# Mixture of experts on one Trainium2 core: the down product from three products of rounded parts in place of float32, and result rows kept in four buffers in place of two

## The reference, cut to what matters

```python
xbuf = jnp.zeros((E, C, D)).at[e_sorted, pos].set(x[tok_sorted], mode='drop')
g = jnp.einsum('ecd,efd->ecf', xbuf, w_gate)
u = jnp.einsum('ecd,efd->ecf', xbuf, w_up)
y = jnp.einsum('ecf,edf->ecd', jax.nn.silu(g) * u, w_down)
y_pair = y[e_sorted, safe_pos] * (s_sorted * valid)[:, None]
out = jnp.zeros((N, D)).at[tok_sorted].add(y_pair)
```

## Time and profile before

| | |
|---|---|
| median of three runs | 2299.77 us (2297.57 to 2302.56) |
| profiled execution, from its first to its last instruction | 2296.0 us |
| what lies around the span, taken as median less span | 3.8 us |
| TensorE busy, over the whole span | 2102.5 us (92%) |
| VectorE busy | 1751.3 us (76%) |
| ScalarE busy | 1441.0 us (63%) |
| POOL busy | 684.0 us (30%) |
| expert stage, from the first transpose to the start of the first load of the last stage | 1864.8 to 2242.9 us |

### The profile page before, as it was taken

The page is one execution under the profiler, slowest core; times in us unless marked ns, Lnnn a source line. Parts: engine busy times, 40 slices in busy tenths (PEclk is TensorE's granted clock), DMA queues, the critical chain, the costliest instruction groups (busy, mean ns, idle before and its releaser), DMA issues. The chain is left out here.

```text
span 2296.0 us, 56054 instructions
## 1 busy us (share of the span) xinstructions
PE 2102.5 (92%) x21448; PEld 1456.2 (63%) x21448; DVE 1751.3 (76%) x3728; ACT 1441.0 (63%) x3012; POOL 684.0 (30%) x646
## 2 busy tenths in 40 slices
PE   7999999999999999999999999999997149999975
PEld 5666666666666666666666666666664037777754
DVE  5557887979797978888888888797978736656646
ACT  2667676768676767676777767676867124444433
POOL 1002040404131322213130404040403427767770
PEclk9999999999999999999999999999999569999998
DMA  7586672323132313232323323232310136676648
GB/s 226 192 288 210 235 250 75 114 82 89 72 89 72 93 70 91 77 83 79 100 88 82 97 64 105 55 105 68 107 47 25 56 119 212 199 229 209 201 138 331
DMA packets 132711, 294.16 MB, mean 128 GB/s; under 512 B 21899, under 2 KB 89143, under 8 KB 126304
## 3 DMA queue, kind: packets, MB, share of 16 engines
q1 hardware_dynamic: 114016, 255.89, 35.7%
q0 software_dynamic: 18432, 34.69, 4.3%
HBM read 165.40 MB, written 108.27 MB: 119 GB/s over the span
## 5 line engine op out<-in xcount | busy, mean ns | idle before, releaser
L801 ACT ACTIVATE sb_probs<-S,sb_negmax 128x1604 f32<-128x1604 f32 x256 | 409.2, 1598 | 278.5 <-DVE sb_negmax L979 277.0
L793 ACT ACTIVATE sb_probsT<-W 128x384 f32<-128x384 f32 (+1 forms) x1024 | 473.6, 513 | 68.2 <-PE W L639 65.3
L639 PE MATMUL W<-sb_ident,sb_probs 128*128 128x128 f32 (+1 forms) x3328 | 478.3, 280 | 15.7 <-DVE sb_o_tok L992 8.0
L979 DVE TENSOR_REDUCE sb_negmax<-S 128x1 f32<-128x1604 f32 x256 | 466.2, 1821 | 2.9 <-PE S L629 1.2
L639 PEld LDWEIGHTS W<-sb_ident,sb_probs 128*128 128x128 f32 (+1 forms) x3328 | 363.5, 139 | 133.9 <-issue 64.7
L612 PE MATMUL W<-sb_wkv_in,sb_ctx 128*128 128x256 f32 (+1 forms) x1664 | 410.7, 389 | 14.2 <-ACT sb_probsT L793 6.6
L602 PE MATMUL W<-sb_ctx,sb_wkv_in 128*32 128x401 f32 x4096 | 399.3, 504 | 4.4 <-DVE sb_V L973 2.9
L612 PEld LDWEIGHTS W<-sb_wkv_in,sb_ctx 128*128 128x128 f32 (+1 forms) x1664 | 293.3, 187 | 79.1 <-ACT sb_probsT L793 25.7
L1335 POOL DMA_INDIRECT y_scratch<-sb_ys,sb_places x256 | 264.4, 1033 | 112.1 <-issue 109.0
L963 DVE SCALAR_TENSOR_TENSOR sb_K_lo<-W,sb_pair_cols,sb_K_hi 128x401 fp32r<-128x401 f32 x256 | 162.2, 633 | 175.5 <-ACT sb_K_hi L785 175.2
L785 ACT ACTIVATE sb_K_hi<-W,sb_pair_cols 128x401 fp32r<-128x401 f32 x256 | 153.2, 598 | 181.5 <-PE W L602 181.4
(11 more groups left out here) (188 smaller groups left out, 2921.0 us busy)
## 6 DMA issues: line engine op xcount, KB each, us to landing
sb_ctx<-ctxT SPq DMA_DIRECT2D x32, 1604.0 KB, 7.7
xe_scratch<-sb_none SPq DMA_DIRECT2D x32, 1088.0 KB, 12.7
sb_xg<-xe_scratch SPq DMA_DIRECT2D x64, 544.0 KB
sb_BC<-bc_scratch SPq DMA_DIRECT2D x32, 1024.0 KB, 5.9
sb_Q_hi<-sb_q_hi SPq DMA_DIRECT2D x128, 128.0 KB, 4.5
sb_Q_lo<-sb_q_lo SPq DMA_DIRECT2D x128, 128.0 KB, 5.4
y_scratch<-sb_none SPq DMA_DIRECT2D x16, 1024.0 KB, 12.0
sb_rows<-y_scratch SPq DMA_DIRECT2D x16, 1024.0 KB, 8.1
```

Source lines behind the costliest of these rows:

```text
L639: ins = pe.transpose(W[0:keys_in(t), at * P:(at + 1) * P], probs[n % 2][:, t * P:t * P + keys_in(t)], ident[:])
L793: act.activation(probsT[k][n % (k + 1)][:, 0:wide], ring[bank_of("T", G, k)][:, 0:wide], ACT.Copy)\
L801: act.activation(probs[n % 2][:].rearrange("p (c k) -> p c k", c=QUADS), scores_of, ACT.Exp, bias=negmax[:, slot:slot + 1], accum_out=den[ ...
L979: dve.tensor_reduce(negmax[:, slot:slot + 1], scores_of, AX.XY, ALU.max, negate=True).then_inc(max_done, 1)
```

## The change

The down product of each expert is made from rounded parts, as gate and up already are. `hid` (now a single float32 tile) is split into `hid_hi` (ScalarE) and `hid_lo` (VectorE), and `wd` into `wd_hi` (ScalarE) and `wd_lo` (VectorE), two buffers each; `down` does three float32r matmuls for each 128 tokens. In ScalarE's order the split stands between silu and `split(e + 1)`, and in VectorE's between `split(e + 1)` and `find_places(e + 1)`. `down` waits for `hid_lo`, and so does SP before it loads the next `wd` into a buffer (it waited for `down`). `ys` has four buffers in place of two, with a semaphore each, so a copy into one waits for the scatters of expert e - 4 in place of e - 2. VectorE's wait for `down` ahead of `hid` is gone, and `hid` is written again only behind its own readers.

```diff
--- before.py
+++ after.py
@@ -1234,6 +1234,7 @@
             return ctx.enter_context(nc.semaphore(name))
 
         X3_AT = E // 2
+        DEEP = 4
         ident = sb("ident2", [P, P])
         xg = [sb(f"xg{n}", [P, CT, XW]) for n in range(2)]
         match = sb("match", [P, CT, TOPK])
@@ -1245,8 +1246,10 @@
         w_hi, w_lo = ([sb(f"w_{m}{n}", [P, DT, 2 * FF], F32R) for n in range(2)] for m in ("hi", "lo"))
         x_hi, x_lo = ([sb(f"x_{m}{n}", [P, DT, CAP], F32R) for n in range(2)] for m in ("hi", "lo"))
         sg = sb("sg", [FF, CAP])
-        hid = [sb(f"hid{n}", [FF, CAP]) for n in range(2)]
-        ys = [sb(f"ys{n}", [P, CT, D]) for n in range(2)]
+        hid = sb("hid", [FF, CAP])
+        hid_hi, hid_lo = ([sb(f"hid_{m}{n}", [FF, CAP], F32R) for n in range(2)] for m in ("hi", "lo"))
+        wd_hi, wd_lo = ([sb(f"wd_{m}{n}", [FF, D], F32R) for n in range(2)] for m in ("hi", "lo"))
+        ys = [sb(f"ys{n}", [P, CT, D]) for n in range(DEEP)]
         XT = [ctx.enter_context(nc.psum_tensor(f"XT{k}", [P, CAP], F32)) for k in range(DT)]
         G = ctx.enter_context(nc.psum_tensor("G", [P, CAP], F32))
         U = ctx.enter_context(nc.psum_tensor("U", [P, CAP], F32))
@@ -1265,9 +1268,12 @@
         gu_done = sem("gu_done")
         sg_up = sem("sg_up")
         hid_up = sem("hid_up")
+        hid_hi_up = sem("hid_hi_up")
+        wd_hi_up = sem("wd_hi_up")
+        down_lo_up = sem("down_lo_up")
         y_done = sem("y_done")
         y_up = [sem("y_up_act"), sem("y_up_dve")]
-        y_out = [sem(f"y_out{n}") for n in range(2)]
+        y_out = [sem(f"y_out{n}") for n in range(DEEP)]
         match_up = sem("match_up")
         place_sum = sem("place_sum")
         places_up = sem("places_up")
@@ -1284,8 +1290,9 @@
         def last(e):
             return isinstance(e, int) and e == E - 1
 
-        def early(e):
-            return isinstance(e, int) and e < 2
+        def rows_out(e):
+
+            return 16 * CT * (e // DEEP)
 
         def in_count(e, n, each=16):
 
@@ -1311,7 +1318,7 @@
 
                 if e == X3_AT:
                     sp.dma_start(dram["x3_sb"][:], dram["x3"].rearrange("(i p) d -> p i d", p=P)).then_inc(dram["x3_in"], 16)
-                after(sp, y_done, e - 1)
+                after(sp, down_lo_up, e - 1)
                 sp.dma_start(wd[n][:], io["wdT"][bass.ds(e, 1)].rearrange("o f d -> (o f) d")).then_inc(wd_in[n], 16)
 
             load_x(0, 0)
@@ -1334,11 +1341,11 @@
                 for c in range(CT):
                     pool.indirect_dma_start(
                         dram["y"], bass.IndirectOffsetOnAxis(ap=places[e % 4][:, c:c + 1], axis=0),
-                        ys[n][:, c, :], None, bounds_check=TOK * TOPK - 1, oob_is_err=False).then_inc(y_out[n], 16)
+                        ys[e % DEEP][:, c, :], None, bounds_check=TOK * TOPK - 1, oob_is_err=False).then_inc(y_out[e % DEEP], 16)
 
             over_experts(pool, body)
-            for n in range(2):
-                pool.wait_ge(y_out[n], 16 * CT * (E // 2))
+            for n in range(DEEP):
+                pool.wait_ge(y_out[n], rows_out(E))
 
 
         @block.tensor
@@ -1366,13 +1373,15 @@
                     ins.then_inc(done, 1)
 
             def down(e, n):
-                pe.wait_ge(hid_up, e + 1)
-                pe.wait_ge(wd_in[n], in_count(e, n))
+                pe.wait_ge(down_lo_up, e + 1)
 
                 for m in range(2):
                     after(pe, y_up[m], e)
+                products = ((hid_hi, wd_hi), (hid_lo, wd_hi), (hid_hi, wd_lo))
                 for c in range(CT):
-                    ins = pe.matmul(Y[c // 2][:, c % 2, :], hid[n][:, c * P:(c + 1) * P], wd[n][:], start=True, stop=True)
+                    for p, (h, w) in enumerate(products):
+                        ins = pe.matmul(Y[c // 2][:, c % 2, :], h[n][:, c * P:(c + 1) * P], w[n][:],
+                                        start=(p == 0), stop=(p == len(products) - 1))
                 ins.then_inc(y_done, 1)
 
             pe.wait_ge(e_const, 2)
@@ -1400,16 +1409,25 @@
                     act.wait_ge(xt_done, DT * e + k + 1)
                     act.activation(x_hi[n][:, k, :], XT[k][:], ACT.Copy).then_inc(x_hi_up, 1)
 
+            def split_down(e, n):
+
+                act.wait_ge(wd_in[n], in_count(e, n))
+
+                after(act, y_done, e - 1)
+                act.activation(wd_hi[n][:], wd[n][:], ACT.Copy).then_inc(wd_hi_up, 1)
+                act.wait_ge(hid_up, e + 1)
+                act.activation(hid_hi[n][:], hid[:], ACT.Copy).then_inc(hid_hi_up, 1)
+
             def out(e, n):
                 act.wait_ge(y_done, e + 1)
-                if not early(e):
-                    act.wait_ge(y_out[n], (e - n) * 8 * CT)
-                act.activation(ys[n][:, 0:2, :], Y[0][:], ACT.Copy).then_inc(y_up[0], 1)
+                after(act, y_out[e % DEEP], rows_out(e))
+                act.activation(ys[e % DEEP][:, 0:2, :], Y[0][:], ACT.Copy).then_inc(y_up[0], 1)
 
             def body(e, n):
                 act.wait_ge(g_done, e + 1)
                 after(act, hid_up, e)
                 act.activation(sg[:], G[0:FF, :], ACT.Silu).then_inc(sg_up, 1)
+                split_down(e, n)
                 if not last(e):
                     split(e + 1, 1 - n)
                 if not first(e):
@@ -1430,6 +1448,13 @@
                     dve.tensor_tensor(x_lo[n][:, k, :], XT[k][:], x_hi[n][:, k, :].bitcast(F32), ALU.subtract)\
                        .then_inc(x_lo_up, 1)
 
+            def split_down(e, n):
+
+                dve.wait_ge(wd_hi_up, e + 1)
+                dve.tensor_tensor(wd_lo[n][:], wd[n][:], wd_hi[n][:].bitcast(F32), ALU.subtract)
+                dve.wait_ge(hid_hi_up, e + 1)
+                dve.tensor_tensor(hid_lo[n][:], hid[:], hid_hi[n][:].bitcast(F32), ALU.subtract).then_inc(down_lo_up, 1)
+
             def find_places(e, n):
 
                 dve.wait_ge(x_in[n], in_count(e, n))
@@ -1437,25 +1462,24 @@
                                          ALU.is_equal, ALU.mult).then_inc(match_up, 1)
                 dve.wait_ge(match_up, e + 1)
                 dve.tensor_reduce(place[:], match[:], AX.X, ALU.add).then_inc(place_sum, 1)
-                if e >= 4:
-                    dve.wait_ge(y_out[n], (e - n - 2) * 8 * CT)
+                after(dve, y_out[e % DEEP], rows_out(e))
                 dve.wait_ge(place_sum, e + 1)
                 dve.tensor_scalar(places[e % 4][:], place[:], float(NO_PLACE), None, ALU.add).then_inc(places_up, 1)
 
             def out(e, n):
                 dve.wait_ge(y_done, e + 1)
-                if not early(e):
-                    dve.wait_ge(y_out[n], (e - n) * 8 * CT)
-                dve.tensor_copy(ys[n][:, 2:4, :], Y[1][:]).then_inc(y_up[1], 1)
+                after(dve, y_out[e % DEEP], rows_out(e))
+                dve.tensor_copy(ys[e % DEEP][:, 2:4, :], Y[1][:]).then_inc(y_up[1], 1)
 
             def body(e, n):
                 dve.wait_ge(gu_done, e + 1)
                 dve.wait_ge(sg_up, e + 1)
 
-                after(dve, y_done, e - 1)
-                dve.tensor_tensor(hid[n][:], U[0:FF, :], sg[:], ALU.mult).then_inc(hid_up, 1)
+                dve.tensor_tensor(hid[:], U[0:FF, :], sg[:], ALU.mult).then_inc(hid_up, 1)
                 if not last(e):
                     split(e + 1, 1 - n)
+                split_down(e, n)
+                if not last(e):
                     find_places(e + 1, 1 - n)
                 if not first(e):
                     out(e - 1, 1 - n)
```

## The result

The changed kernel takes **2377.77 us** (median of five runs, 2376.23 to 2380.77) against 2299.77: a ratio of 1.0343, with a 95% interval of 1.0331 to 1.0354. It is 78 us slower, where the prediction said 69.

The account below looks back on a forecast made before the run. Bound: TensorE's work and the chain hid, w_lo, x_lo, gate, nearly equal. Sum: 62 x (6.69 - 5.552) = +70.6, first expert +1.2, end -2.9, so +69 on 2296.0, plus 3.8: 2369 us, range 2356 to 2388.

Parts of the forecast that it names:

- The bound of before: Expert loop: TensorE's work and the path hid, w_lo, x_lo, gate end within a tenth of each other, period 5.47 us.
- The new link in the chain: ScalarE: w_hi and x_hi stand behind hid_hi's wait for hid; next gate at 3.67 against 2.45, +1.22 us per expert.
- Down product: TensorE: twelve one-pass matmuls take 1.4 to 2.6 us against 1.73, low end taken (0.118 each); shortening buys nothing.
- Loads, "I cost this at nothing": SP's queue: wd is wanted earlier by wd_hi but is issued in the previous expert's turn; no cost counted.
- The cover of 5 us: wd load: lands some 5 us ahead of its use; without that, a late wd delays silu's successors and w_hi equally.
- End of the stage, -2.9: From last hid to last scatter, 14.72 us before: eight scatters follow, the last near 11.8; -2.9 us, bounds -6 and 0.
- Four buffers: ys: they end the Y copy's wait for scatters, 55 us that were nearly all off the path.
- the 5 us of hiccups: Expert loop: 62 x 0.08 = 5 us above the flat period, counted as gone by using 6.69 flat.
- A: Rival, faster: TensorE's work is the bound and hid's split hides in ScalarE's idle time; about 2270 us, 4 in 100.
- B: Rival: TensorE's rests drop its clock from 2.4 to 1.2 GHz, 175 us on top, 2544 us; 2 in 100.
- C: Rival: scatters in progress hold VectorE, wd_lo and hid_lo each losing up to 0.97 us; 60 more, 2429 us; 3 in 100.
- the stretch is on POOL's side only: Subtractions beside scatters: the trace shows only POOL lengthened; two more cost POOL perhaps 0.4 us per expert, VectorE nothing.

Follow-up runs that it names:

- hid_hi late: The changed kernel with hid_hi moved on ScalarE behind w_hi and x_hi of the next expert: 2303.04 us, ratio 1.0016 to the kernel before.
- the doubled copy: The changed kernel with a second copy of hid on ScalarE, into a tile nothing reads, right before hid_hi: 2427.68 us.

## Why the prediction was right, point by point

- *The bound of before*: right. With the split of hid off the path and a shorter down product, the period stayed at 5.48 us (hid_hi late); the chain hid, w_lo, x_lo held it, with TensorE's full row hiding that. With the chain off the path, it fell to 5.10.
- *The new link in the chain*: right, step by step. Counted from the start of hid (2002.73), hid_hi started at 0.72 (0.73 forecast), w_hi at 1.25 (1.25), w_lo at 1.80 (1.80), x_lo at 2.28 (2.28), the next gate product at 3.67 (3.67). Moving hid_hi alone undid it.
- *Down product*: the low end was right, 0.119 us a matmul (0.118), and it bought nothing in this order, as said.
- *Loads, "I cost this at nothing"*: mis-sized. The cover of 5 us did hold in every turn but one; at the big load it was gone, and that measured 4.8 us by the two periods, 1.3 of them in the turn at 1.2 GHz, of which moving the load gave back 3.1 in the loop. The prediction named the cost of a lost cover but did not look at what SP issues between the loads at expert 32, though the kernel before has its longest turn of the loop there (8.16 us).
- *End of the stage, -2.9*: mis-sized. From the last hid to the last scatter it is 13.94 us in place of 14.72, so -0.8. The sum let POOL begin with expert 62 after the last hid. In fact it was still scattering expert 61 then, as the copy of Y for expert 61 stands behind all of VectorE's work for 62. Twelve scatters, not eight, lay behind it:

```profile
2301.73 0.97 POOL L1342 DMA_INDIRECT y_scratch<-sb_ys,sb_places  x1 [1.84 <-DVE sb_ys L1472]
...
2301.84 0.69 DVE L1478 TENSOR_TENSOR sb_hid<-U,sb_sg 96x512 f32<-96x512 f32 x1 [0.97 <-PE U L1371]
...
2315.78 0.97 POOL L1342 DMA_INDIRECT y_scratch<-sb_ys,sb_places  x1 [0.30 <-issue]
```

- These two terms (4.8 and 2.1), the 2.8 by which the stage began later and 0.9 behind the last scatter, less 0.3 in the rest, make up the 79.2 - 69 = 10 us between the forecast and the span. The 2.8 and the 0.9 lie in code that is the same in both. Apart from the late wd the loop took (419.5 - 4.8) / 62 = 6.69 us a turn, as forecast.
- *Four buffers*: right that they are worth next to nothing; alone they gave 0.9994. But they did not take the 5 us of hiccups away, which the sum counted as gone: most of these lie at the big load, where the turn stays at 7.36 us in the kernel with the buffers alone, and in the changed kernel the late wd took their place.
- *The rivals*: A fell at the place that was named, since w_hi starts after hid ends (2003.98 and 2003.42). B did not happen (granted clock 1.00 in the loop, but for the turn behind the late wd), though the doubled copy shows that it was near. C fell: hid_lo with its two SBUF inputs took 678 to 690 ns in all 64 cases, and w_lo 557 to 559, while scatters ran beside them. That the stretch is on POOL's side only was too strong, though. In the changed kernel the short step that writes the places took 0.41 us in place of 0.17 in 5 of 64 turns, ending within 0.01 us of the end of a scatter that it fell into; and with the doubled copy wd_lo took 0.48 in place of 0.41 in most turns, where a scatter started inside it. The exclusion that the Trainium skill states on the page SBUF — State Buffer, section Who interferes with whom, shows on VectorE's side in such pieces of at most 0.3 us here, and in no run as a wait for a whole scatter.

## What to carry to other kernels

On an engine that takes its instructions in order, look at what stands behind a new wait before pricing the new work: a copy of 0.63 us that nobody was in a hurry for cost 75 of the 78 us, because the next expert's first step stood behind it, and they came back when that copy was moved. Shortening the busiest engine gains nothing while a chain through two other engines ends at the same time; find by how much each path ends ahead of the next one, here the chain at 5.48 us, POOL at 5.3 to 5.4, TensorE at 5.10. When a load is wanted earlier than before, go through the queue for the one turn in which something big stands in front of it.

## What had not been expected of the hardware

TensorE's clock held at 2.4 GHz through rests of 1.41 us in every 6.70, and fell to 1.2 GHz for some 3 us in 11 of 62 turns with rests of 1.92 us in every 7.21, though it was busy for 8.08 of 10 us in both stretches shown above. In that one kernel, half a microsecond more of rest per turn cost 33 us, and the clock 14 us on top.
